# A two-layer decoder on one core: two evictions given to VectorE around silu, a context rounding a round later, the gated feed-forward layer transposed, unread matmuls in the last division

## The chip, the cores and the metric

The kernel runs on 1 core of one Trainium2 chip. The metric is device time in microseconds (us). Before the change it is 509.97 us, the median of 3 runs (506.48 to 510.33).

## What is computed

Two decoder layers over x of 8 batches x 56 tokens x 256 features. The parts of the reference that matter here, cut:

```python
# layer 0, cross attention over ctx_2048 (8 x 1500 x 256), 16 heads of 16
q, k, v = proj(hs, Wq, bq, S), proj(at, Wk, bk, T), proj(at, Wv, bv, T)
scores = clip(einsum('bhsd,bhtd->bhst', q, k) / 4, -50, 50)   # masked keys: -50
probs = softmax(scores)
delta = einsum('bhst,bhtd->bhsd', probs, v) @ Wo.T + bo
# layer 0, gated feed-forward, 256 -> 1024 -> 256, on quantised activations and ternary weights
gate = einsum('bsh,oh->bso', act_quant(x), weight_quant(w_gate))
up   = einsum('bsh,oh->bso', act_quant(x), weight_quant(w_up))
intermediate = silu(gate) * up
out = einsum('bsh,oh->bso', act_quant(fwht(intermediate)), weight_quant(w_down))
# act_quant: per token, scale = 128 / max|x|, round, clip; fwht: Walsh-Hadamard over 1024
```

Ahead of it stands self attention of layer 0 (16 heads of 128); behind it attention of layer 1 across the batches, a summary of the context, and a second feed-forward layer (h, a lookup of gelu, out).

## The kernel before

The 448 tokens are four divisions of 112 (`NT`, `TT`), t = 0 to 3; each holds two batches. Each engine runs a program written out by hand, with semaphores between them.

**Stages.** Warm-up matmuls and the first normalisation (to about 9 us of the span), self attention of layer 0 over 16 heads (to about 130 us), then the cross attention in 48 rounds (`PAIRS`), s = 0 to 47, of 250 context rows each; two rounds make a unit u = s // 2 of 500 rows, six rounds a batch. What stands behind cross attention for division t (its output projection, the gated feed-forward, layer 1) is cut into steps and woven into the rounds: `early(t, o)` and `late(t, o)` run step o of division t in round s = 12(t + 1) + o. Division 3 has no rounds left, so its steps, with what is left of divisions 0 to 2, make a serial last stretch from 428 us to the end.

**A round on TensorE (PE).** `scores(s)` (L1469, into `psa`); `project_k` for the next unit (L1398, into the bank `kvb` of `psb`); `weighted_values(s - 1)` (L1487, into `pvb`); early steps; `project_vu` for the next unit (L1408, also into `kvb`); late steps. As keys and values use one bank, `project_k` waits until the values before have been evicted (`s_vue`), and `project_vu` until the keys have (`s_ke`).

**ScalarE (ACT)** takes `exponential(s)` (L624), `move_k` (L460: keys out of `kvb`), in even rounds `round_up(u + 2)` (L389: the context rounded to fp32r), early steps, `move_vu` (L467: values out of `kvb`), late steps. In rounds 16, 28 and 40 it also runs `silu(t)` for t = 0, 1, 2: it loads another activation table (L502), takes silu of the gate bank (L505), and after `move_vu`, in late step 4, loads the first table back (L508).

**VectorE (DVE)** takes `remainder` (L820: context minus its rounded part, in odd rounds), early steps, `clip(s)` (L983), `weigh` (L959), late steps.

**The gated feed-forward of division t**, before: quantised tokens are transposed (L1520) and evicted (L499, `xqT`); late step 3 (round 15 for t = 0) multiplies them with the gate weights, tokens on the partitions, 4 matmuls of 512 columns (L1526); round 16 takes silu; early step 5 (round 17) multiplies with the up weights (L1526, 4 more; it waits for silu, as it overwrites the gate's banks); late step 5 multiplies both on DVE (`times_up`, L1026); butterflies in rounds 17 and 18 do three of the ten Hadamard stages over blocks of 128 features (L1034, L1035); late step 6 (round 18) transposes the 8 blocks (`turn_inter`, L1547) and ACT evicts them (`move_hT`, L512); early step 7 (round 19) multiplies by the 128 x 128 Hadamard matrix (L1553); the rest (scale, round, down projection) fills rounds 19 to 21. Division 3 does the same in the last stretch in halves (L1706, L1712, L662, L1229, L1720, L669, L1726).

`keep_warm(n)` issues n matmuls of 128 x 512 (L1678) whose result nobody reads.

## Time and profile before

| | |
|---|---|
| runs | 509.97, 506.48, 510.33 us (median 509.97) |
| the profiled execution | 506.57 us, of which the span from first to last instruction is 504.8 us |
| mean granted TensorE clock | 0.993 |
| PE busy | 476.2 us (94%) |
| DVE busy | 357.7 us (71%) |
| ACT busy | 330.3 us (65%) |

How to read it: the span is that of one profiled execution; a matmul's end is modelled, so the distance from one group of matmuls to the next is the better measure of what it costs. The granted clock is the share of full speed at which TensorE was allowed to run: 1.0 is 2.4 GHz and 0.5 is 1.2 GHz. A time in brackets behind a row is how long the engine stood idle before it, with what released it.

### The profile page before, as it was taken

Reading aid. Unit: us, or ns where it says so; the run is one execution under the profiler, and the core shown is the slowest. Engines: PE = TensorE matmul, PEld = TensorE weight load, DVE = VectorE, ACT = ScalarE, POOL = GpSimd, SP = SyncE. Lnnn points to the kernel's source line nnn. Section 1 sums busy time; section 2 is a strip of 40 time slices with the busy share of each in tenths; the row PEclk is TensorE's granted clock in tenths of the full one; section 3 lists DMA queues with packets and bytes.
Section 4 is the critical chain, followed back from the end, with each engine's and each line's share of the span. In section 5 each row is a group of like instructions: output and inputs, shape, how many; then the busy total and the mean of one; then the engine's idle time right before and its main releaser. Section 6 shows DMA issues by size and latency. Waiting matters only on the chain.

```text
span 504.8 us, 16223 instructions
## 1 busy us (share of the span) xinstructions
PE 476.2 (94%) x6980; PEld 404.2 (80%) x6986; DVE 357.7 (71%) x805; ACT 330.3 (65%) x600; POOL 4.2 (1%) x15
## 2 busy tenths in 40 slices
PE   8999999999898999999999998999999899887897
PEld 7999999998787888886878877788877687665575
DVE  5666887888475764673856587955978865698973
ACT  4777787879465656668566667766667756264744
POOL 1000000000000000000000000000000000000000
PEclk9999999999999999999999999999999999799999
DMA  6567451203202111111111111111111100000000
GB/s 195 145 234 258 141 160 39 62 23 123 108 16 70 43 44 44 43 43 43 43 44 43 44 43 43 43 43 44 44 43 44 43 3 3 1 2 1 1 9 29
DMA packets 12236, 30.85 MB, mean 61 GB/s; under 512 B 1667, under 2 KB 4868, under 8 KB 11397
## 3 DMA queue, kind: packets, MB, share of 16 engines
q1 hardware_dynamic: 11716, 29.08, 18.2%
q8 instruction: 56, 0.92, 0.7%
q0 software_dynamic: 192, 0.51, 0.3%
q10 hardware_dynamic: 256, 0.23, 0.1%
q14 instruction: 16, 0.12, 0.1%
HBM read 29.35 MB, written 0.46 MB: 59 GB/s over the span
## 4 chain that ended last, share of the span: by engine, by line
PE 69%; DVE 16%; ACT 10%; issue 4%; DMA 1%; SPq 0%; ACTq 0%; DVEq 0%
PE psb L1408 10%; PE psb L1398 10%; PE psa L1469 8%; PE psa L1317 7%; PE psb L1487 5%; PE psa L1330 4%; PE pst L1339 3%; PE psb L1370 3%; PE psa L1350 2%; ACT shared L624 2%; PE psa L1747 1%; PE pst L1553 1%; PE psb L1361 1%; DVE smem L983 1%; ACT smem L624 1%
## 5 line engine op out<-in xcount | busy, mean ns | idle before, releaser
L1408 PE MATMUL psb<-wkv,cx 128*125 128x256 f32 x576 | 80.4, 288 | 2.8 <-ACT kx L460 2.8
L1398 PE MATMUL psb<-cx,wkv 128*128 128x500 f32 x276 | 74.5, 405 | 4.2 <-ACT vmem L467 4.2
L1408 PEld LDWEIGHTS psb<-wkv,cx 128*125 128x125 f32 x576 | 71.0, 186 | 6.4 <-ACT kx L460 4.9
L467 ACT ACTIVATE vmem<-psb 125x512 f32<-125x512 f32 x48 | 28.6, 596 | 55.9 <-PE psb L1408 55.9
L1398 PEld LDWEIGHTS psb<-cx,wkv 128*128 128x128 f32 x276 | 48.3, 188 | 16.2 <-ACT vmem L467 4.9
L983 DVE TENSOR_SCALAR shared<-shared,top 125x896 f32<-125x896 f32 x48 | 30.8, 684 | 35.8 <-ACT shared L624 35.5
L1469 PE MATMUL psa<-qb,kx 32*125 32x112 f32 x1536 | 54.7, 279 | 0.8 <-ACT shared L624 0.6
L1469 PEld LDWEIGHTS psa<-qb,kx 32*125 32x125 f32 x1536 | 46.3, 183 | 9.3 <-issue 4.6
L983 DVE TENSOR_SCALAR smem<-smem,top 125x896 f32<-125x896 f32 x48 | 30.8, 683 | 27.1 <-ACT smem L624 27.1
L624 ACT ACTIVATE smem<-psa 125x1792 f32<-125x1792 f32 x24 | 40.0, 1666 | 12.3 <-PE psa L1469 12.3
L624 ACT ACTIVATE shared<-psa 125x1792 f32<-125x1792 f32 x24 | 40.0, 1666 | 10.5 <-PE psa L1469 10.3
L1317 PE MATMUL psa<-cx 128*128 128x448 f32 x192 | 43.0, 373 | 0.8 <-DVE cx L792 0.8
L1317 PEld LDWEIGHTS psa<-cx 128*128 128x128 f32 x192 | 34.8, 188 | 3.6 <-DVE cx L792 1.0
L460 ACT ACTIVATE kx<-psb,cols_sb 128x500 f32<-128x500 f32 x46 | 30.9, 672 | 2.3 <-PE psb L1398 2.3
L959 DVE CUSTOM_DVE_ANT_0 scratch<-ring,cw 128x500 f32<-128x500 f32 x48 | 32.3, 673 | 0.0
L373 ACT ACTIVATE shared<-shared,negmax 112x112 f32<-112x112 f32 x64 | 24.1, 378 | 9.2 <-DVE negmax L860 9.2
L820 DVE TENSOR_TENSOR cx<-ring,cx 128x1000 fp32r<-128x1000 f32 x24 | 28.7, 1195 | 2.0 <-ACT cx L389 1.8
L1487 PEld LDWEIGHTS psb<-smem,vmem 125*32 125x32 f32 x1536 | 20.4, 110 | 7.9 <-issue 7.8
L1487 PEld LDWEIGHTS psb<-shared,vmem 125*32 125x32 f32 x1536 | 20.3, 110 | 8.0 <-issue 7.7
L389 ACT ACTIVATE cx<-ring 128x1000 fp32r<-128x1000 f32 x24 | 25.0, 1041 | 2.4 <-DMA ring<-ctx_t_dram 2.4
L1330 PE MATMUL psa<-wkv,cx 128*112 128x256 f32 x192 | 25.2, 280 | 0.0
L1330 PEld LDWEIGHTS psa<-wkv,cx 128*112 128x112 f32 x192 | 24.4, 174 | 0.7
(337 smaller groups left out, 823.9 us busy)
## 6 DMA issues: line engine op xcount, KB each, us to landing
ring<-ctx_t_dram SPq DMA_DIRECT2D x24, 500.0 KB, 3.5
whd<-wqk_dram SPq DMA_DIRECT2D x16, 256.0 KB, 2.7
qb<-wvp_dram SPq DMA_DIRECT2D x8, 256.0 KB, 2.9
whd<-wo_dram SPq DMA_DIRECT2D x16, 128.0 KB, 2.7
wraw<-w_dram SPq DMA_DIRECT2D x2, 1024.0 KB, 5.9
mats_sb<-mats_dram SPq DMA_DIRECT2D x1, 1536.0 KB, 9.0
wraw<-gate_dram SPq DMA_DIRECT2D x1, 1024.0 KB, 6.3
wraw<-up_dram SPq DMA_DIRECT2D x1, 1024.0 KB, 6.9
```

The costliest lines, as they stand in the source:

```text
L460: nc.scalar.activation(kx[u % 2][:, m, :], bank[:, 0:UT], ACT.Identity, bias=cols_sb[:, 1, m:m + 1]).then_inc(s_ke, 1)
L467: nc.scalar.activation(vu[u % 2][:, 2 * r:2 * r + 2, :, 0:XD], bank[0:CT, :].rearrange("p (t h d) -> p t h d", t=2, d=XD), ACT.Copy).then_ ...
L624: nc.scalar.activation(ex[s % 2], psa[0:CT, :, 0:448], ACT.Exp, scale=0.25).then_inc(s_ex, 1)
L820: nc.vector.tensor_tensor(cx[LO][u % 2][:, :, :], ctxs[u % 3], cx[HI][u % 2][:, :, :].bitcast(F32), ALU.subtract).then_inc(s_cx, 1)
L959: nc.vector.tensor_tensor_reduce(out=wscr[:, c, :], in0=ctxs[u % 3][:, c, :], in1=cw[:, (u % UPB) * UT:(u % UPB + 1) * UT], scale=1.0, sca ...
L983: nc.vector.tensor_scalar(half, half, top[:, pp // 2 // UPB, key:key + 1], 1.0 / ECLIP, ALU.min, ALU.max).then_inc(s_clip, 1)
L1317: last = nc.tensor.matmul(PS[0][:, part, 0:TOK], cq[a][h % 2][:, (c * 2 + part) * P:(c * 2 + part + 1) * P], x0[b][:, c, :], start=(a == b ...
L1330: last = nc.tensor.matmul(A2[0:TT, i * D:(i + 1) * D], x0[b][:, c, t * TT:(t + 1) * TT], wkv[a][:, j % 2, c, :], start=(a == b and c == 0) ...
L1398: last = nc.tensor.matmul(bank[:, 0:UT], wkv[a][:, 0, c, m * P:(m + 1) * P], cx[b][u % 2][:, c, :], start=(a == b and c == 0), stop=(a == ...
L1408: last = nc.tensor.matmul(bank[0:CT, t * D:(t + 1) * D], cx[b][u % 2][:, c, a0:a0 + CT], wkv[a][:, 1, c, :], start=(a == b and c == 0), st ...
L1469: last = nc.tensor.matmul(psa[0:CT, g, t * 224 + c * 112:t * 224 + (c + 1) * 112], kx[u % 2][32 * g:32 * g + 32, c, a0:a0 + CT], qb[32 * g ...
L1487: last = nc.tensor.matmul(pvb[32 * i:32 * i + 32, q * S:(q + 1) * S], vu[u % 2][:, 2 * r + t, 4 * q + i, :], ex[pp % 2][:, g, a0:a0 + S], ...
```

## The change

1. **Evictions around silu.** In rounds 16, 28 and 40 (`SILU`) the values, and in the rounds after them (17, 29, 41, `BEHIND`) the keys, are evicted by DVE (`take_vu`, `take_k`) and not by ACT. `round_up` of rounds 16, 28, 40 is done by ACT in the round after, and so is `remainder`, which DVE now does behind `weigh` and not at the round's head.
2. **Transposed layer.** The gate and the up projection now have features on the partitions and tokens in the columns (`widen`: 16 matmuls of 128 x 112 each for the 4 of 512 columns). `turn_inter` and `move_hT` are gone; the Hadamard matmuls read the butterflies' output. The scale of the gate, one number for each token, is now one for each column: `spread_scale` (a matmul) copies it to all partitions, `move_gB` (ACT) evicts it, and `scale_gate` (DVE) multiplies it in and writes the gate to SBUF. So the up projection no longer waits for silu, only for `scale_gate`, and moves from early step 5 to late step 4, a round earlier. The scale of up goes into the quantiser's numbers.
3. **Last division.** The last exponential is cut in two halves; `weighted_values(46)` goes ahead of `project_qkv(2)`; 3 and 4 unread matmuls are added around the transposes of the context; `keep_weighted(7)` goes behind `spread`.
4. **Start.** 18 fp32 warm-up matmuls of 128 x 128 become 6 of these, 8 in fp32r and 16 of 32 x 112; one semaphore (`s_rest`) is merged into another.

```diff
+SILU = (16, 28, 40)
+BEHIND = (17, 29, 41)
...
-        inter = whd[1][0:TT, 0:FF]
-        butt = scratch[0:TT, FF:2 * FF]
+        inter = whd[1][:, 0:FC * TT]
+        butt = scratch[:, FF:FF + FC * TT]
+        gB = sb("gB", [P, TT])
...
+            def move_gB(t):
+                act.wait_ge(s_gb, t + 1)
+                nc.scalar.activation(gB[:, :], (A1 if t == 3 else T1)[:, 0:TT], ACT.Copy).then_inc(s_gbe, 1)
+
             def silu(t):
                 nc.scalar.preload_act_table(ACT.Silu)
-                act.wait_ge(s_gu, t + 1)
-                act.wait_ge(s_gate, t + 1)
-                nc.scalar.activation(sil, both, ACT.Silu, scale=gu[:, t, 0:1]).then_inc(s_sil, 1)
+                act.wait_ge(s_gs, t + 1)
+                nc.scalar.activation(sil, sil, ACT.Silu).then_inc(s_sil, 1)
...
                 exponential(s)
-                if s >= 2 and u + 1 < B * UPB:
+                if s >= 2 and s not in BEHIND and u + 1 < B * UPB:
                     move_k(u + 1, r, kvb)
-                if r == 0 and u + 2 < B * UPB:
+                if (s in BEHIND or r == 0 and s not in SILU) and u + 2 < B * UPB:
                     round_up(u + 2)
...
-                if u + 1 < B * UPB:
+                if s not in SILU and u + 1 < B * UPB:
                     move_vu(u + 1, r, kvb)
...
-            exponential(PAIRS - 1)
+            act.wait_ge(s_qk, PAIRS)
+            act.wait_ge(s_pv, PAIRS - 2)
+            for t in range(2):
+                nc.scalar.activation(ex[1][:, :, t * 224:(t + 1) * 224], psa[0:CT, :, t * 224:(t + 1) * 224], ACT.Exp, scale=0.25).then_inc(s_ex, 1)
...
+            def take_k(u, m):
+                dve.wait_ge(s_kp, 2 * u + m + 1)
+                dve.wait_ge(s_qk, 2 * u - 2)
+                nc.vector.tensor_scalar_add(kx[u % 2][:, m, :], kvb[:, 0:UT], cols_sb[:, 1, m:m + 1]).then_inc(s_ke, 1)
+
+            def take_vu(u, r):
+                dve.wait_ge(s_vp, 2 * u + r + 1)
+                dve.wait_ge(s_pv, 2 * (u - 2) + r + 1)
+                nc.vector.tensor_copy(vu[u % 2][:, 2 * r:2 * r + 2, :, 0:XD], kvb[0:CT, :].rearrange("p (t h d) -> p t h d", t=2, d=XD)).then_inc(s_vue, 1)
...
+            def scale_gate(t):
+                dve.wait_ge(s_gate, t + 1)
+                dve.wait_ge(s_gbe, t + 1)
+                nc.vector.tensor_tensor(in_banks(sil), wide_T, gB[:, :].unsqueeze(1).unsqueeze(1).to_broadcast([P, 2, 4, TT]), ALU.mult).then_inc(s_gs, 1)
...
+                if o == 4:
+                    scale_gate(t)
                 if o == 6:
                     butterfly(t, 1)
...
             for s in range(PAIRS - 2):
-                if s % 2 and s // 2 + 2 < B * UPB:
+                if s in BEHIND:
+                    take_k(s // 2 + 1, 1)
+                elif s % 2 and s // 2 + 2 < B * UPB:
                     remainder(s // 2 + 2)
...
                 weigh(s // 2, s % 2)
+                if s in SILU:
+                    take_vu(s // 2 + 1, s % 2)
+                if s in BEHIND:
+                    remainder(s // 2 + 2)
...
-            for _ in range(18):
+            for _ in range(6):
                 nc.tensor.matmul(T0[:, 0:P], ones[:, :], ones[:, :], start=True, stop=True)
+            for _ in range(8):
+                nc.tensor.matmul(T0[:, 0:P], rounded[:, :], rounded[:, :], start=True, stop=True)
+            for k in range(16):
+                g = 32 * (k % 4)
+                nc.tensor.matmul(PS[k % 4][:, 0, 0:TT], rounded[g:g + 32, :], rounded[g:g + 32, 0:TT], start=True, stop=True, tile_position=(g, 0))
...
+            def spread_scale(t):
+                pe.wait_ge(s_gu, t + 1)
+                if 0 < t < 3:
+                    pe.wait_ge(s_x4d, t)
+                nc.tensor.matmul((A1 if t == 3 else T1)[:, 0:TT], gu[:, t, 0:1].to_broadcast([TT, P]), ident[0:TT, 0:TT], start=True, stop=True).then_inc(s_gb, 1)
+
+            def widen(n, half, bank):
+                for f in range(4 * half, 4 * half + 4):
                     for c in range(DC):
-                        last = nc.tensor.matmul(pst[0:TT, half, :], xqT[:, c, :], wter[:, n, c * FF + half * 512:c * FF + half * 512 + 512],
+                        last = nc.tensor.matmul(bank[:, (f % 4) * TT:(f % 4 + 1) * TT], wter[:, n, c * FF + f * P:c * FF + (f + 1) * P], xqT[:, c, :],
                                                 start=(c == 0), stop=(c == DC - 1))
...
-                if o == 5:
-                    gate_up(t, 1)
...
-                if o == 6:
-                    turn_inter(t)
+                if o == 4:
+                    gate_up(t, 1)
...
+            weighted_values(PAIRS - 2)
             project_qkv(2)
-            weighted_values(PAIRS - 2)
             weighted_values(PAIRS - 1)
+            keep_warm(3)
             turn_context(3)
             nc.tensor.matmul(A3[0:TT, 0:D], minus[:, :], bias2[:, 0:D], start=True, stop=False)
+            keep_warm(4)
             turn_divided(3)
```

The order of the programs around division 1's silu, rounds 28 and 29. ACT before: L624 is the exponential, L460 the keys, L389 `round_up`, L329 and L333 a normalisation's root, L502 and L508 the table loads, L505 silu, L467 the values.

```order
L624 ACTIVATE shared<-psa 125x1792
L460 ACTIVATE kx<-psb,cols_sb 128x500
L389 ACTIVATE cx<-ring 128x1000
L329 ACTIVATE lnv<-mv,eps 112x1
L333 ACTIVATE y<-lnv 112x1
L502 ACT_TABLE_LOAD
L505 ACTIVATE whd<-pst,gu 112x1024
L467 ACTIVATE vmem<-psb 125x32x16
L508 ACT_TABLE_LOAD
L329 ACTIVATE lnv<-mv,eps 112x1
L333 ACTIVATE y<-lnv 112x1
L624 ACTIVATE smem<-psa 125x1792
```

ACT after, the same place (L626 the exponential, L464 the keys, L393 `round_up`, L510 and L515 the table loads, L512 silu, L471 the values).

```order
L626 ACTIVATE shared<-psa 125x1792
L464 ACTIVATE kx<-psb,cols_sb 128x500
L333 ACTIVATE lnv<-mv,eps 112x1
L337 ACTIVATE y<-lnv 112x1
L510 ACT_TABLE_LOAD
L512 ACTIVATE whd<-whd 128x896
L515 ACT_TABLE_LOAD
L333 ACTIVATE lnv<-mv,eps 112x1
L337 ACTIVATE y<-lnv 112x1
L626 ACTIVATE smem<-psa 125x1792
L393 ACTIVATE cx<-ring 128x1000
L471 ACTIVATE vmem<-psb 125x32x16
```

The rounding and the values have left the round of silu, and the next exponential is followed by the rounding and not by the keys.

DVE after, from `clip(28)` to `remainder(16)`, with the short instructions of a normalisation between them left out where the dots stand: L986 `clip`, L960 `weigh`, L997 `take_vu`, L992 `take_k`, L820 `remainder`.

```order
L986 TENSOR_SCALAR shared<-shared,top 125x4x224 x2
L960 ISA scratch,wb<-ring,cw 128x500
L960 ISA wb 128x1
L997 COPY vmem<-psb 125x32x16
...
L992 TENSOR_SCALAR kx<-psb,cols_sb 128x500
L786 SCALAR_TENSOR_TENSOR yt<-y,nx 112x1
L788 SCALAR_TENSOR_TENSOR rs<-yt,y 112x1
L1156 TENSOR_SCALAR wraw<-xs,mv,rs 112x256
L986 TENSOR_SCALAR smem<-smem,top 125x4x224 x2
L960 ISA scratch,wb<-ring,cw 128x500
L960 ISA wb 128x1
L820 TENSOR_TENSOR cx<-ring,cx 128x1000
```

Before, L820 of this unit stood ahead of the same normalisation and of the second `clip`, and the two evictions were not there.

PE before, from the gate matmuls of round 27 to the scores of round 31 (L1469 scores, L1398 keys, L1487 weighted values, L1408 values, L1621 a transpose of layer 1, L1547 `turn_inter`):

```order
L1526 MATMUL pst<-wter,xqT 112x512 x4
L1469 MATMUL psa<-qb,kx 125x112 x16
L1398 MATMUL psb<-cx,wkv 128x500 x6
...
L1487 MATMUL psb<-shared,vmem 32x56 x32
L1526 MATMUL pst<-wter,xqT 112x512 x4
L1408 MATMUL psb<-wkv,cx 125x256 x12
...
L1621 MATMUL pst<-cst,wraw 128x112 x2
L1408 MATMUL psb<-wkv,cx 125x256 x12
L1547 MATMUL pst<-cst,whd 128x112 x8
L1469 MATMUL psa<-qb,kx 125x112 x16
```

PE after (L1506 scores, L1435 keys, L1524 weighted values, L1445 values, L1564 `spread_scale`, L1569 gate and up, L1659 the transpose):

```order
L1564 MATMUL pst<-cst,gu 128x112
L1557 MATMUL pst<-identb,xq 128x112 x2
L1445 MATMUL psb<-wkv,cx 125x256 x12
L1569 MATMUL pst<-xqT,wter 128x112 x16
L1506 MATMUL psa<-qb,kx 125x112 x16
...
L1445 MATMUL psb<-wkv,cx 125x256 x12
L1569 MATMUL pst<-xqT,wter 128x112 x16
L1506 MATMUL psa<-qb,kx 125x112 x16
...
L1659 MATMUL pst<-cst,wraw 128x112 x2
L1445 MATMUL psb<-wkv,cx 125x256 x12
L1506 MATMUL psa<-qb,kx 125x112 x16
```

The second projection has moved from the middle of round 29, between the weighted values and the values, to the end of round 28, and nothing stands between the values and the scores at the end of round 30.

## Rows read from the trace of the kernel before

**Rows 1.** The page's chain that ended last, share of the span by engine.
```profile
PE 69%; DVE 16%; ACT 10%; issue 4%; DMA 1%; SPq 0%; ACTq 0%; DVEq 0%
```

**Rows 2.** Stretches: length, busy us (instructions) of PE, PEld, DVE, ACT, POOL, clock, DMA.
```profile
228.05:253.79 25.74, 24.45 (x486) 20.25 (x485) 16.80 (x30) 17.07 (x17) 0.00 (x0) 1.00 0.17 49
305.92:332.49 26.57, 24.64 (x488) 20.42 (x487) 20.98 (x45) 18.08 (x22) 0.00 (x0) 1.00 0.17 50
305.92:311.06 5.14, 5.14 (x115) 4.32 (x114) 3.83 (x12) 3.88 (x6) 0.00 (x0) 1.00 0.33 103
311.06:319.24 8.18, 6.29 (x119) 4.77 (x118) 5.46 (x15) 6.45 (x8) 0.00 (x0) 1.00 0.01 2
```

**Rows 3.** Timeline of rounds 28 and 29: start us, us, engine, line, operation, [idle before].
```profile
309.25 1.05 ACT L389 ACTIVATE cx<-ring 128x1000 fp32r<-128x1000 f32 x1
310.73 1.28 ACT L502 ACT_TABLE_LOAD   x1
312.02 1.11 ACT L505 ACTIVATE whd<-pst,gu 112x1024 f32<-112x1024 f32 x1
313.03 0.59 ACT L467 ACTIVATE vmem<-psb 125x512 f32<-125x512 f32 x1
313.64 1.28 ACT L508 ACT_TABLE_LOAD   x1
313.68 1.62 PE L1398 MATMUL psb<-cx,wkv 128*128 128x500 f32 x6 [1.47 <-ACT vmem L467]
317.64 1.68 PE L1408 MATMUL psb<-wkv,cx 128*125 128x256 f32 x12 [0.41 <-ACT kx L460]
```

**Rows 4.** Timeline, TensorE: gate of division 1, its two groups of transposes, scores behind.
```profile
304.96 1.02 PE L1526 MATMUL pst<-wter,xqT 128*112 128x512 bf16 x4
...
324.69 0.98 PE L1547 MATMUL pst<-cst,whd 112*128 112x112 f32 x8
325.61 1.14 PE L1469 MATMUL psa<-qb,kx 32*125 32x112 f32 x32
...
338.49 0.57 PE L1560 MATMUL pst<-identb,mats_sb 112*128 112x112 bf16 x8 [0.35 <-DVE mats_sb L1048]
338.99 1.14 PE L1469 MATMUL psa<-qb,kx 32*125 32x112 f32 x32
```

**Rows 5.** Groups by line and form: xcount | busy us, mean ns of one | idle before.
```profile
L815 DVE COPY vmem<-psa 112x512 f32<-112x512 f32 x16 | 11.1, 692 | 6.1 <-PE psa L1330 5.8
L1026 DVE SCALAR_TENSOR_TENSOR scratch<-pst,gu,whd 112x1024 f32<-112x1024 f32 x3 | 3.9, 1284 | 0.1
L1408 PEld LDWEIGHTS psb<-wkv,cx 128*125 128x125 f32 x576 | 71.0, 186 | 6.4 <-ACT kx L460 4.9
```

**Rows 6.** Timeline, VectorE from round 27 to round 29.
```profile
304.43 0.67 DVE L959 CUSTOM_DVE_ANT_0 scratch<-ring,cw 128x500 f32<-128x500 f32 x1
...
307.38 0.42 DVE L1128 TENSOR_TENSOR xs<-xs,rows_sb 112x256 f32<-112x256 f32 x1
...
308.90 1.28 DVE L983 TENSOR_SCALAR shared<-shared,top 125x896 f32<-125x896 f32 x2 [1.10 <-ACT shared L624]
...
312.58 1.20 DVE L820 TENSOR_TENSOR cx<-ring,cx 128x1000 fp32r<-128x1000 f32 x1
```

**Rows 7.** Timeline, last stretch: the same matmuls for division 3 and later.
```profile
436.04 1.91 PE L1766 MATMUL psa<-mats_sb,xnT 128*112 128x256 f32 x4 [0.24 <-issue]
438.06 0.43 DVE L777 BATCH_NORM_STATS2 st<-psa 112x6 f32<-112x256 f32 x1 [2.25 <-PE psa L1766]
...
468.67 1.12 PE L1822 MATMUL psa<-mats_sb,xnT 128*112 128x256 f32 x4
```

**Rows 8.** Stretch of the last part at the lower clock; columns as in group 2.
```profile
434.90:441.60 6.70, 6.46 (x21) 5.01 (x22) 4.10 (x12) 1.94 (x9) 0.00 (x0) 0.50 0.00 0
```

**Rows 9.** Timeline, TensorE at the start: warm-up and first transposes.
```profile
0.99 6.08 PE L1304 MATMUL pst<-ones 128*128 128x128 f32 x36 [0.99 <-POOL magic L304]
7.74 1.12 PE L1299 MATMUL psb<-cst,xn 112*128 112x112 f32 x8 [0.67 <-DVE xn L767]
```

128 lines of the change are left out of this document (55 added, 73 removed).

## The prediction

> **What bounds the kernel now.** I read the page's chain first, then stretches of whole rounds, then the timeline where a round is longer than its neighbours. The chain that ended last runs over TensorE for 69% of the span [rows 1], so a gain must shorten what TensorE issues, or take away a wait of it. In the 48 rounds a plain one takes 5.14 us and TensorE is busy through it; the round behind a silu takes 8.18 us, of which it is busy 6.29 [rows 2]. Round 29 has a plain round's work and the up projection, whose 4 matmuls of 512 columns take 0.96 us (from 304.96 to the next round's start at 305.92) [rows 2, 4]. That is 6.10, so 2.08 us are lost to waits. The timeline names them: ACT runs `round_up` (1.05), a table load (1.28), silu (1.11), only then the values that `project_k` waits for (TensorE idle 1.47), and a second load (1.28) pushes the exponential and the keys back (idle 0.41) [rows 3]. Rounds 28 to 31 take 26.57 us together, 16 to 19 take 25.74 [rows 2]; the work of division 1 in them is that of division 0, so the wait behind silu is 0.83 less there, 1.25 us. Rounds 40 to 43 repeat 28 to 31. Behind 428 us the last stretch runs in small dependent steps.
>
> **Start of the sum.** The profiled execution: 506.57 us. It is one of the fast ones; the runs' median is 3.4 above it.
>
> **1. The transposed layer on TensorE.** Each division loses 8 transposes, 0.92 us from their first to the scores behind [rows 4]. Gate and up become 16 pairs of a 128-column weight load and 112 columns each. Nearest: 8 bf16 transposes of 112 columns, each with its load, take 338.99 - 338.49 = 0.50 us, 62 ns a pair [rows 4], so 1.00 us for 0.96: +0.08 for both. Lower bound: nothing. Upper bound: the fp32r loads of 125 columns, 186 ns each if none overlaps [rows 5]. `spread_scale` is one fp32 matmul of 112 columns; 2 such of 256 take 1.12 us [rows 7], so about 0.2 (bounds 0.1 and 0.5). Together -0.92 + 0.08 + 0.2 = -0.64 us a division. All of it counts, since TensorE is busy there.
>
> What a page says against the transposed form is set apart here. The Trainium skill ("TensorE: Matmul & The Clock Gate", section "Back-to-back issue gap") gives about 81 ns for a matmul of 128 columns with its weight load; the row has 62. By the page's figure the 8 groups of 16 (two in each of four divisions) would cost 8 x 16 x 0.019 = 2.4 us more.
>
> **2. The waits behind silu.** ACT's rounds 28 and 29 lose the values (0.59) and the keys, `round_up` goes behind the second exponential, and silu sees 896 columns. With the values on DVE, `project_k` of round 29 no longer waits for ACT: `clip` and `weigh` of round 28 end before the values are in the bank, and the copy takes 0.69 [rows 5]. Silu hides behind the rest of round 28, as the up projection, now at that round's end, waits for `scale_gate` only. So 1.25 + 2 x 2.08 us go.
>
> What is late next is DVE's queue. I count from the start of round 28 (0); durations without a group are rounded from the same timeline. `scale_gate` waits for the gate and reads 896 columns: 1.28 x 896 / 1024 = 1.12 [rows 5], so it ends at 1.25. Behind it stands layer 1's normalisation of division 0, which before ran from 305.1, where `weigh` ended, to 307.80, 2.7 us [rows 6]: to 4.0. `clip` 1.28, `weigh` about 0.7: to 5.95. `take_vu` waits for values at about 5.1: to 6.6. The next normalisation, about 1.8: to 8.4. Round 29 starts at 5.14 + 1.0 = 6.15, and its keys are there at 6.15 + 1.07 + 1.55 = 8.8 (scores and keys as in the timeline of every plain round); `take_k` to 9.6, just when the weighted values end (9.75), so no wait. ACT's root for that normalisation ends only at about 8.7, and its exponential (1.67) behind it at 10.4, where before it began at once. `clip`, `weigh`: to 12.4. `remainder` 1.20 [rows 6]: to 13.6. But `project_k` of round 30, which reads it, could start at 6.15 + 5.15 + 1.07 = 12.4. I therefore charge a new wait of 1.15 us in rounds 30 and 42, bounds 0 (if the normalisations slip into gaps) and 2.1 (the old wait in full). In round 18 no normalisation of an earlier division is in the way: the same count ends at 12.8 against 12.4, and I charge 0.5.
>
> DVE's new work (1.12 + 0.69 + 0.7 a division, less an eighth of `times_up` and of six butterflies) is otherwise hidden: DVE is busy 20.98 of 26.57 us in these rounds [rows 2]. It costs once it exceeds the rest, about 5 us.
>
> Loop: divisions 1 and 2: -0.64 - 2.08 + 1.15 = -1.57 each; division 0: -0.64 - 1.25 + 0.5 = -1.39. Sum **-4.5 us**.
>
> **3. The last stretch.** From 434.9 to 441.6 TensorE has half of its clock [rows 8]. There the output projection of division 3 takes 1.91 us where the same shape takes 1.12 later, and DVE waits 2.25 us for it [rows 7]. What the clock did before: TensorE stood with gaps around the context's transposes. The 7 unread matmuls, a quarter of 0.96 us each [rows 4], lie in waits for DVE's `take_raw` and `divide`, so they delay nothing. If the clock stays up, 0.8 us of the projection leave the path, and I estimate 0.45 (between 0 and 0.8) for the small matmuls ahead of it, which ran at the same clock: -1.25. Against it `scale_gate` stands in two halves behind the wide `total` on DVE, +1.1, and gives back an eighth of the product and the butterflies, -0.65; the transposes' eviction was hidden by DVE. Halved exponential and earlier weighted values: -0.1. That is -0.9 with the clock up, rounded to **-1.0 us**, and +0.35 without; I take -1.0, since the added matmuls stand just ahead of the fall.
>
> **4. The start.** Shorter warm-ups gain nothing: TensorE waits for `xn`, ready at 7.74 whatever it did before [rows 9]. Merging a semaphore takes no instruction away but a wait. Price: 0, upper bound in rival C.
>
> **Sum.** 506.57 - 4.5 - 1.0 = 501.07, so **501.0 us**. The median of the runs shown is 509.97, 1.8% above that; a cause of their two levels (506.5 and 510) is not in this profile, and I don't forecast that it goes.
>
> **Rivals.**
> - **A, DVE's queue takes the whole gain.** `take_k` and `take_vu` are queued in order behind normalisations that wait for ACT; if keys or values come late as well as the remainder, each division keeps its old wait, and only the removed transposes are left: 506.57 - 3 x 0.64 - 1.0 = 503.6; with more waits in rounds 17 to 19, up to 507. For: the count above has 0.2 us of slack at the keys. Against: DVE is busy 5.46 of 8.18 us in round 29 [rows 2].
> - **B, weight loads don't overlap (slower).** At p ns a pair the 8 groups cost 128 x (p - 62). The point of no gain is 5.5 us / 128 + 62 = 105 ns. At the 186 ns of the fp32r load [rows 5] it is +15.9, so 517. Against: the loads in rows 4 do overlap, with bf16 weights as here.
> - **C, a slow start.** The warm-ups end some 2 us earlier (6 of 18 fp32 matmuls are 2.0 of 6.08 us; the 24 others are short), so TensorE idles about 2.5 us rather than 0.67 before its first transposes [rows 9]. If it then has half its clock as long as in rows 8, some 5.5 us of matmuls take 1.7 times as long (1.91 / 1.12): +3.9 at most, 504.9; half hidden, 503.
> - **D, the change doesn't do what it says**: the clock falls in the last stretch all the same: 502.4.
>
> **How the numbers follow.** The forecast with D (one answer): 0.58, between 497.5 (no new wait: 3.0 less, and some of the lost time elsewhere) and 503.5. A 0.18, 503 to 507. C 0.14, 502 to 505. B 0.10, of which half above 515. The range 497 to 507 leaves out B and a little at the low end: also in it is a median on the upper of the two levels (501 + 3.4 = 504.5). About 1% is what a measurement of this kernel can tell from no change; against 509.97 faster means below 504.9: the forecast nearly whole, C's larger and A's smaller part, 0.76. Within 1%: 0.18. Slower: 0.06.
>
> **What would show it.** In the changed profile: rounds 17, 29 and 41 at 5.2 us, rounds 16, 28 and 40 at 6.2; `project_k` of rounds 30 and 42 waiting about 1.1 us for DVE's `remainder` (none in A's place would be a gain more; waits for `take_k` or `take_vu` speak for A); 16 matmuls of the gate in 1.0 us (B: over 1.7); no `turn_inter`; a granted clock of 1.0 around 435 us (D: 0.5) and from 7 to 12 us (C: 0.5). I am wrong if the 12 rounds around the silus together are not 3 to 7 us shorter than their 78.9.

## The result, and the profile of the changed kernel

| | before | changed |
|---|---|---|
| median, us (executions) | 506.44 (20) | 504.10 (20) |
| lowest to highest | 504.98 to 510.33 | 502.77 to 506.83 |
| profiled execution | 506.57 | 502.77 (span 501.0) |
| first scores of the loop | 140.38 | 142.20 |
| loop, first to last scores | 286.30 | 281.38 |
| last scores to the end of the span | 78.1 | 77.4 |

The ratio is 0.995, with a 95% interval of 0.9929 to 0.9972. The changed kernel is 2.3 us (0.5%) faster; forecast was 5.5 us below before's profiled execution, 501.0. The three executions of before shown ahead of the forecast had a median of 509.97; twenty give 506.44, so that 3.5 of the 9 us between 510 and 501 were never there; of the other 5.4 us the change brought 2.3. The profiled executions differ by 3.8 us, and the table's lower rows say where: loop -4.92, last stretch -0.7, start +1.82.

The chain that ended last, by engine, answers to [rows 1]: ACT has lost half of its share to TensorE and DVE.

```profile
PE 71%; DVE 18%; ACT 5%; issue 4%; DMA 1%; DVEq 0%; ACTq 0%
```

Rounds 28 to 31 of the changed kernel, as stretches (length, then busy us of PE, PEld, DVE, ACT, POOL, clock, DMA share, GB/s), answering to [rows 2]:

```profile
306.25:312.20 5.95, 5.95 (x132) 5.12 (x131) 5.56 (x14) 4.68 (x6) 0.00 (x0) 1.00 0.28 85
312.20:317.39 5.19, 5.19 (x117) 4.33 (x115) 4.32 (x13) 4.44 (x6) 0.00 (x0) 1.00 0.02 5
317.39:323.74 6.35, 5.33 (x117) 4.48 (x116) 6.18 (x12) 4.13 (x5) 0.00 (x0) 1.00 0.28 83
323.74:330.91 7.17, 6.95 (x131) 6.05 (x130) 6.98 (x14) 2.84 (x3) 0.00 (x0) 1.00 0.08 10
sum 24.66, PE 23.42 PEld 19.99 DVE 23.05 ACT 16.09 POOL 0.00; mean PE 5.86 PEld 5.00 DVE 5.76 ACT 4.02 POOL 0.00
```

They take 24.66 us for 26.57. Round 29 has lost its 2.08 us of waits. What waits now is round 30, and DVE is busy through 23.05 of the 24.66 us, where it was 20.98 of 26.57. The timeline of the same rounds names the operations, answering to [rows 3] and [rows 4]:

```profile
311.31 0.96 PE L1569 MATMUL pst<-xqT,wter 128*128 128x112 bf16 x16
311.42 0.95 ACT L512 ACTIVATE whd<-whd 128x896 f32<-128x896 f32 x1
313.27 1.62 PE L1435 MATMUL psb<-cx,wkv 128*128 128x500 f32 x6
...
319.55 1.58 PE L1435 MATMUL psb<-cx,wkv 128*128 128x500 f32 x6 [1.02 <-DVE cx L820]
...
326.66 0.99 PE L1524 MATMUL psb<-shared,vmem 125*32 125x56 f32 x64 [0.22 <-DVE craw L977]
```

`project_k` of round 29 (313.27) waits for nothing; that of round 30 (319.55) waits 1.02 us for DVE's `remainder`. New besides is a small wait in round 31 for `take_raw` (L977, the context's copy `craw`).

At the start the changed kernel's first matmuls are slower than those of [rows 9]. Timeline of TensorE, then the stretch behind its warm-ups:

```profile
0.99 2.93 PE L1336 MATMUL pst<-ones 128*128 128x128 f32 x12 [0.99 <-POOL magic L308]
3.57 1.95 PE L1338 MATMUL pst<-ones 128*128 128x128 f32 x8
...
7.67 1.73 PE L1330 MATMUL psb<-cst,xn 112*128 112x112 f32 x8 [1.11 <-DVE xn L768]
10.12 4.13 PE L1354 MATMUL psa<-cx 128*128 128x448 f32 x12 [0.72 <-ACT cx L362]
```

```profile
7.40:14.00 6.60, 5.61 (x20) 4.92 (x21) 3.63 (x8) 4.09 (x8) 1.77 (x3) 1.00 0.65 199
```

The transposes take 1.73 us for 1.12 and the first 12 matmuls of `project_qk` 4.13 for 2.77. The granted clock of the stretch is shown as 1.00 all the same. That is no record: the first record of the clock in this trace begins at 13.34 us of the span (in the kernel before at 4.78 us), and the view counts time without a record as full speed. The distances between the starts of instructions say what the clock was. In the changed kernel's fp32 and rounded warm-ups they are 0.21 us to the end, and in `project_qk` 0.37 us up to 13.3 us and 0.20 behind it; in the kernel before, those of the warm-ups fall from 0.21 to 0.11 us at 4.8 us. So the changed kernel's TensorE was not at full speed in its warm-ups, which end at 6.55 us, nor before 13.3 us.

In the last stretch the clock no longer falls at 434.9 [rows 8], 8.2 us behind the last scores, but at 440.0, 16.4 us behind them, over gate and up of division 3. The output projection, then the gate, then both stretches:

```profile
432.25 1.02 PE L1787 MATMUL psa<-mats_sb,xnT 128*112 128x256 f32 x4
433.38 0.43 DVE L778 BATCH_NORM_STATS2 st<-psa 112x6 f32<-112x256 f32 x1 [0.41 <-PE psa L1787]
440.25 1.67 PE L1569 MATMUL pst<-xqT,wter 128*128 128x112 bf16 x16 [0.45 <-ACT xqT L503]
```

```profile
434.90:439.90 5.00, 3.10 (x22) 2.04 (x20) 4.51 (x17) 2.90 (x7) 0.00 (x0) 1.00 0.01 2
440.20:443.60 3.40, 3.35 (x35) 3.35 (x35) 3.13 (x7) 1.54 (x3) 0.00 (x0) 0.53 0.00 0
```

The projection takes 1.02 us for 1.91, and DVE waits 0.41 us for it, not 2.25 [rows 7].

### The profile page after: what moved, and what is told of

It reads as the page before. It is cut to its first block, busy times and chain, and to the rows that moved or that the text cites. A ratio compares the mean times of both kernels' runs of the same rounds, so it can differ in the third digit from the quotient of the medians.

```text
span 501.0 us, 16404 instructions
## 1 busy us (share of the span) xinstructions
PE 474.7 (95%) x7067; PEld 406.3 (81%) x7067; DVE 363.4 (73%) x817; ACT 324.2 (65%) x594; POOL 4.3 (1%) x15
## 4 chain that ended last, share of the span: by engine, by line
PE 71%; DVE 18%; ACT 5%; issue 4%; DMA 1%; DVEq 0%; ACTq 0%
PE psb L1445 11%; PE psb L1435 10%; PE psa L1506 8%; PE psa L1354 7%; PE psb L1524 6%; PE psa L1367 4%; PE pst L1376 4%; PE psb L1407 3%; PE psa L1387 2%; ACT shared L626 2%; PE psa L1766 1%; PE pst L1569 1%; DVE scratch L960 1%; PE pst L1591 1%; DVE shared L986 1%
## 5 line engine op out<-in xcount | busy, mean ns | idle before, releaser
L1445 PE MATMUL psb<-wkv,cx 128*125 128x256 f32 x576 | 80.2, 288 | 2.2 <-ACT kx L464 2.2
L1435 PE MATMUL psb<-cx,wkv 128*128 128x500 f32 x276 | 74.4, 405 | 2.5 <-DVE cx L820 2.2
L1445 PEld LDWEIGHTS psb<-wkv,cx 128*125 128x125 f32 x576 | 71.0, 186 | 4.7 <-ACT kx L464 2.9
L471 ACT ACTIVATE vmem<-psb 125x512 f32<-125x512 f32 x45 | 26.8, 596 | 53.3 <-PE psb L1445 53.3
L1435 PEld LDWEIGHTS psb<-cx,wkv 128*128 128x128 f32 x276 | 48.3, 188 | 14.4 <-issue 2.7
L1506 PE MATMUL psa<-qb,kx 32*125 32x112 f32 x1536 | 54.7, 279 | 0.8 <-ACT shared L626 0.6
L986 DVE TENSOR_SCALAR shared<-shared,top 125x896 f32<-125x896 f32 x48 | 30.8, 685 | 31.5 <-ACT shared L626 31.2
L1506 PEld LDWEIGHTS psa<-qb,kx 32*125 32x125 f32 x1536 | 46.3, 183 | 8.2 <-issue 3.4
L626 ACT ACTIVATE smem<-psa 125x1792 f32<-125x1792 f32 x23 | 38.4, 1669 | 12.8 <-PE psa L1506 12.8
L626 ACT ACTIVATE shared<-psa 125x1792 f32<-125x1792 f32 x24 | 40.0, 1665 | 10.4 <-PE psa L1506 10.1
L1354 PE MATMUL psa<-cx 128*128 128x448 f32 x192 | 44.4, 382 | 0.7 <-ACT cx L362 0.7
L986 DVE TENSOR_SCALAR smem<-smem,top 125x896 f32<-125x896 f32 x48 | 30.8, 682 | 19.1 <-ACT smem L626 18.5
L1354 PEld LDWEIGHTS psa<-cx 128*128 128x128 f32 x192 | 36.1, 195 | 3.7 <-DVE cx L793 1.0
L960 DVE CUSTOM_DVE_ANT_0 scratch<-ring,cw 128x500 f32<-128x500 f32 x48 | 32.3, 673 | 0.0
L464 ACT ACTIVATE kx<-psb,cols_sb 128x500 f32<-128x500 f32 x43 | 28.9, 673 | 4.2 <-PE psb L1435 3.9
L820 DVE TENSOR_TENSOR cx<-ring,cx 128x1000 fp32r<-128x1000 f32 x24 | 28.7, 1195 | 1.9 <-ACT cx L393 1.8
L1524 PEld LDWEIGHTS psb<-shared,vmem 125*32 125x32 f32 x1536 | 20.4, 110 | 9.0 <-issue 6.7
L1524 PEld LDWEIGHTS psb<-smem,vmem 125*32 125x32 f32 x1536 | 20.3, 110 | 8.0 <-issue 7.8
L393 ACT ACTIVATE cx<-ring 128x1000 fp32r<-128x1000 f32 x24 | 24.9, 1037 | 2.4 <-DMA ring<-ctx_t_dram 2.3
```

The lines of the kernel that those rows point to most:

```text
L464: nc.scalar.activation(kx[u % 2][:, m, :], bank[:, 0:UT], ACT.Identity, bias=cols_sb[:, 1, m:m + 1]).then_inc(s_ke, 1)
L471: nc.scalar.activation(vu[u % 2][:, 2 * r:2 * r + 2, :, 0:XD], bank[0:CT, :].rearrange("p (t h d) -> p t h d", t=2, d=XD), ACT.Copy).then_ ...
L626: nc.scalar.activation(ex[s % 2], psa[0:CT, :, 0:448], ACT.Exp, scale=0.25).then_inc(s_ex, 1)
L820: nc.vector.tensor_tensor(cx[LO][u % 2][:, :, :], ctxs[u % 3], cx[HI][u % 2][:, :, :].bitcast(F32), ALU.subtract).then_inc(s_cx, 1)
L960: nc.vector.tensor_tensor_reduce(out=wscr[:, c, :], in0=ctxs[u % 3][:, c, :], in1=cw[:, (u % UPB) * UT:(u % UPB + 1) * UT], scale=1.0, sca ...
L986: nc.vector.tensor_scalar(half, half, top[:, pp // 2 // UPB, key:key + 1], 1.0 / ECLIP, ALU.min, ALU.max).then_inc(s_clip, 1)
```

## The experiments

Times are medians, with lowest, highest and number of executions; ratios are to the kernel before on the same chip, whose median there was 506.40 to 506.69. "Changed" is the kernel of the result. "12 rounds" are 16 to 19, 28 to 31 and 40 to 43 together.

| kernel | us | ratio, 95% | loop starts | loop | 12 rounds |
|---|---|---|---|---|---|
| before | 506.44 | | 140.38 | 286.30 | 78.9 |
| changed | 504.10 | 0.995 | 142.20 | 281.38 | 73.2 |
| e1_old_warmup | 501.37 (500.64 to 502.53, 6) | 0.9877 to 0.9923 | 140.37 | 281.41 | 73.2 |
| e2_before_new_warmup | 508.28 (507.39 to 511.08, 12) | 1.0022 to 1.0059 | 142.28 | 285.98 | 78.9 |
| e4_layer_only | 506.34 (505.70 to 509.61, 12) | 0.9981 to 1.0017 | 142.47 | 283.07 | 75.0 |
| e5_evictions_only | 504.88 (503.97 to 507.89, 12) | 0.9956 to 0.9992 | 140.48 | 284.84 | 77.6 |
| e3_no_unread | 503.33 (501.31 to 507.29, 12) | 0.9905 to 0.9956 | 140.35 | 285.00 | 73.2 |
| e7_more_unread | 502.75 (501.01 to 505.46, 8) | 0.9890 to 0.9944 | 140.46 | 285.14 | 73.2 |
| e6_dve_order | 501.63 (501.48 to 504.17, 6) | 0.9878 to 0.9938 | 140.42 | 281.74 | 72.2 |
| e9_short_warmup | 506.19 (502.27 to 507.71, 10) | 0.9933 to 0.9994 | 142.91 | 284.19 | 73.2 |
| e8_long_rounded | 505.25 (500.48 to 506.26, 8) | 0.9902 to 0.9975 | 145.10 | 281.02 | 73.2 |
| e11_filled_wait | 503.36 (502.14 to 504.11, 6) | 0.9912 to 0.9961 | 142.64 | 281.51 | 73.2 |
| e12_split_wait | 501.59 (501.12 to 501.78, 4) | 0.9865 to 0.9931 | 140.34 | 281.27 | 73.2 |
| e13_all | 499.29 (499.10 to 499.85, 5) | 0.9833 to 0.9883 | 140.37 | 279.69 | 70.1 |

### The start: e1 and e2

```diff
 pe.wait_ge(s_init, 1)
-for _ in range(6):                      # fp32, then 8 + 16 rounded ones
+for _ in range(18):                     # fp32 only, as before
     nc.tensor.matmul(T0[:, 0:P], ones[:, :], ones[:, :], start=True, stop=True)
```

`e1_old_warmup` is the changed kernel with the old warm-ups; `e2_before_new_warmup` the kernel before with the new ones.

> The changed kernel with the 18 fp32 warm-up matmuls of before; all else as changed. Theory (the start pays): in the changed kernel's trace the first 8 transposes take 1.73 us and not 1.12, and the first values of self attention start at 14.09 us and not 12.31; with the old warm-ups they are back near 12.3, the loop's first scores near 140.4, and the time falls by about 1.8 us against the changed kernel. Rival (the late start is chance, or comes from another edit such as the merged semaphore): the first values still start near 14.1 in part of the executions, and the median stays within 0.5 us of the changed kernel's 504.1.

> The kernel before with the changed kernel's warm-ups (6 fp32, 8 fp32r, 16 of 32 x 112); all else as before. Theory (the start pays): the first transposes take about 1.7 us, the first values start near 14.1 us, and the time rises by about 1.8 us over before. Rival (chance, or another edit): no change beyond 0.5 us.

The timeline of TensorE in e1:

```profile
7.71 1.07 PE L1330 MATMUL psb<-cst,xn 112*128 112x112 f32 x8
9.62 2.78 PE L1348 MATMUL psa<-cx 128*128 128x448 f32 x12 [0.84 <-DVE cx L793]
```

The start is the old one, and e1 takes 501.37 us, 2.7 less than the changed kernel. In e2 the transposes take 1.73 us and the loop starts at 142.28; the kernel before becomes 1.7 us slower. So the new warm-ups cost 1.8 to 1.9 us at the loop's start in a profiled execution, with either loop, and the rest of the change is worth the 5.2 us that lie between 506.59 (before beside e1) and 501.37.

### Length or kind of the warm-ups: e9 and e8

```diff
-for _ in range(18):                     # e9: fp32 alone, but shorter
+for _ in range(11):
```

```diff
 for _ in range(6): ...                  # e8: fp32, as in the changed kernel
-for _ in range(8):                      # rounded, 128 columns
+for _ in range(28):
     nc.tensor.matmul(T0[:, 0:P], rounded[:, :], rounded[:, :], start=True, stop=True)
-for k in range(16): ...                 # the small ones
```

> The changed kernel with 11 fp32 warm-up matmuls: the old kind of work, which ends at about the time at which the new mixture ended (6.5 us), so that TensorE idles as long ahead of its first transposes. If the idle time ahead of the transposes is what lowers the clock, the first transposes take 1.7 us for 1.1 and the loop's first scores stand at 142.2 as in the changed kernel (504.1 - about 503.5 us). If the kind of the warm-ups counts (the 24 small ones), the start is as in e1: transposes 1.07, loop's first scores 140.4, 501.4 us.

> The changed kernel with warm-ups of the new kind (6 fp32 matmuls, then fp32r ones: 28 instead of 8, and none of the 16 small ones), so that they last as long as the old ones. If the idle time ahead of the first transposes is the cause of the slow start, this start is the old one: transposes 1.07 to 1.12 us, first values at 12.2 to 12.3, the loop's first scores at 140.4, 501 to 501.7 us. If the kind counts (the row of the changed kernel shows a granted clock of 1.00 there, though its matmuls take 1.5 times as long), transposes stay at 1.73 and the loop's first scores at about 142.2.

TensorE in e9, where it stands idle for 2.04 us, and its stretch behind:

```profile
7.71 1.27 PE L1330 MATMUL psb<-cst,xn 112*128 112x112 f32 x8 [2.04 <-DVE xn L768]
```

```profile
8.60:15.30 6.70, 5.97 (x19) 5.06 (x19) 3.16 (x6) 3.67 (x8) 0.70 (x2) 0.50 0.72 222
```

TensorE in e8, where it is not idle at all, and its stretch behind:

```profile
3.58 6.21 PE L1338 MATMUL pst<-ones 128*128 128x128 f32 x28
9.59 1.72 PE L1330 MATMUL psb<-cst,xn 112*128 112x112 f32 x8
```

```profile
9.40:14.00 4.60, 3.88 (x15) 3.35 (x15) 2.31 (x5) 2.01 (x4) 0.00 (x0) 1.00 0.58 196
```

Each theory shows in a kernel of its own. In e9 the warm-ups reach full speed at 5.1 us, TensorE then stands idle for 2.04 us, and the clock falls at 8.5 us, during the transposes: with warm-ups at full speed, idle time alone makes the start slow. (The median of e9 is no price of this. Its executions stand in two groups, four at 502.3 to 503.1 us and six at 506.1 to 507.7, and the profiled one, of the upper group, loses time in round 2 as well, as told below.)

In e8 there is no idle time, and the transposes take 1.72 us nevertheless; the 28 rounded matmuls started 0.21 us apart, so they themselves ran slowly to their end at 9.8 us (which also delayed the transposes by 1.9 us, for which I had not allowed: I had taken their price from too short a row). The first record of the clock begins at 17.2 us there, so the 1.00 of its stretch is again no record. Of e8's eight executions three took 500.5 to 500.7 us and five 504.6 to 506.3. One of the five was profiled; that the three reached full speed in their warm-ups fits their times, but is not shown.

In the nine profiles with fp32 warm-ups alone, full speed was reached at 4.8 to 7.0 us. In the five with rounded ones it was reached at 3.9 us once (e11, below), and otherwise not before 13.2 us. As the changed kernel's warm-ups end at 6.55 us, within the range of the nine, it may be enough that they are short; that their kind matters too rests on e8 alone.

### What the unread matmuls of the last division do: e3 and e7

```diff
 weighted_values(PAIRS - 1)
-keep_warm(3)                            # e3: neither
 turn_context(3)
 ...
-keep_warm(4)
 turn_divided(3)
```

```diff
-keep_warm(4)
+keep_warm(8)                            # e7: longer, and 2 more
 spread_scale(3)
+keep_warm(2)
 turn_xq(3)
```

Both on top of e1.

> The changed kernel with the old warm-ups (as e1_old_warmup, 501.37 us) and without the 3 + 4 unread matmuls of the last division. If those hold the clock there, as I forecast, the granted clock falls earlier, near 435 us on the old count, and the output projection of division 3 takes 1.9 us for 1.1: the forecast's terms (-1.25 with the clock held, none without) give up to +1.25, so 501.7 to 502.6. In the changed kernel the clock fell anyway, at about 440 us, for 3.4 us of the records; if the unread matmuls only shift a fall that comes in any case, the fall is longer or sits over other work, and I expect +0.3 to +0.8. Rival: they change nothing, since TensorE's gaps ahead of the fall come from other places; then within 0.2 us of e1 and the same stretches at half clock.

> The changed kernel with the old warm-ups and two longer blocks of unread matmuls: 8 for 4 while DVE normalises ahead of the gate of division 3, and 2 more behind spread_scale(3). In the changed kernel TensorE stands idle from about 437.2 to 440.2 and is then at half clock until about 443.8; gate and up of division 3 take 1.67 and 1.70 us there, where 16 such pairs take 0.8 to 1.0 in the loop. If the idle time ahead brings the fall, the clock stays up over gate and up: about 0.7 of each pair of stretches, of which the up projection hides partly behind DVE's scale_gate, so -0.5 to -0.9 us against e1's 501.37. Rival: the added matmuls run past the moment at which the gate could start (8 of a quarter of 0.96 us are 1.9 us), and delay what they should help: 0 to +0.5.

Stretches around gate and up of division 3 and, for e1 and e7, some 14 us later. First e1, then e3, then e7:

```profile
438.40:441.80 3.40, 3.40 (x48) 3.40 (x49) 3.30 (x8) 1.81 (x3) 0.00 (x0) 1.00 0.00 0
452.80:456.40 3.60, 3.29 (x17) 2.48 (x18) 2.89 (x7) 1.97 (x4) 0.00 (x0) 0.61 0.01 2
```

```profile
441.90:445.40 3.50, 3.47 (x36) 3.48 (x37) 3.40 (x8) 1.88 (x3) 0.00 (x0) 0.56 0.00 0
```

```profile
442.20:445.60 3.40, 3.39 (x48) 3.39 (x49) 3.30 (x8) 1.80 (x3) 0.00 (x0) 1.00 0.00 0
455.60:459.00 3.40, 2.66 (x16) 2.23 (x17) 2.71 (x6) 2.39 (x5) 0.00 (x0) 0.56 0.01 2
```

In each profile of the new last division the clock falls for 3.4 us once or twice there: over the gate, some 14 us later, or at both places, as in e3, whose second fall is at 456.0 us. The unread matmuls don't decide where. The changed kernel, e8, e11, e12 and e13 have the last division of e1, and their clock falls over the gate as it does in e3; in e12 it falls at both places. Its stretch over the gate:

```profile
439.40:442.70 3.30, 3.30 (x26) 3.30 (x24) 3.20 (x8) 2.61 (x4) 0.00 (x0) 0.50 0.00 0
```

Nor does the place matter much: `scale_gate` begins 17.49 to 17.53 us behind the last scores in e1, e3 and e7, whether the gate takes 0.96 or 1.36 us, since the last stretch is DVE's there. From the last scores to the end it is 77.7 us in e1, 78.1 in e3, 78.0 in e7. But the profiles with e1's own last division run from 77.3 us (e11, e13) to 78.4 (e12), so neither taking the unread matmuls away nor adding more has an effect that these profiles could tell from nothing. My expectation of -0.5 to -0.9 for e7 was wrong: it took the changed kernel's slow gate as given, and in e1 the gate ran in 0.96 us without the added matmuls.

In e3 the projection takes 1.02 us as in the changed kernel, so it isn't the 7 unread matmuls of the last division that moved the fall away from 434.9. Nor is it the warm-ups: in e2 the clock falls 8.2 us behind the last scores, as before. What did lies in the part of the change that e4 has and e5 has not (both below), as the stretch behind 434 us shows, first of e5, then of e4:

```profile
433.30:440.20 6.90, 6.90 (x24) 5.21 (x24) 4.41 (x12) 2.26 (x9) 0.00 (x0) 0.52 0.00 0
```

```profile
433.50:440.50 7.00, 5.76 (x37) 4.32 (x37) 5.96 (x21) 3.65 (x11) 0.00 (x0) 1.00 0.01 2
```

That is the rewritten last division, and within it, by e3, not the 7 matmuls; the halved exponential, the earlier weighted values and the later `keep_weighted(7)` are what is left ahead of that place, untested.

The medians of e3 and e7 are 1.4 to 2 us above that of e1, and their profiled executions 4. Almost all of the 4 us is one place outside the change, which the next section treats.

### Round 2, and the spread between executions: e11

In the profiles of e3 and e7 rounds 2 and 3 take 3.6 and 3.7 us more than in e1. The reason stands in the timelines: a transfer of the context lands late, ACT's rounding behind it too, and TensorE waits longer for ACT's `xnT`. ACT begins that rounding at 153.12 us in e1 and 0.55 us later in e3. ACT and TensorE in e3, and TensorE's stretch behind:

```profile
153.67 1.04 ACT L393 ACTIVATE cx<-ring 128x1000 fp32r<-128x1000 f32 x1 [2.92 <-DMA ring<-ctx_t_dram]
155.01 1.54 PE L1457 MATMUL pst<-xnT,mats_sb 128*128 128x112 f32 x8 [2.07 <-ACT xnT L478]
```

```profile
155.60:161.60 6.00, 6.00 (x59) 4.64 (x62) 4.13 (x12) 1.92 (x2) 0.00 (x0) 0.50 0.01 3
```

In the kernel before this wait was 1.53 us, in the changed one 1.49, in e1, e2, e4, e5 and e6 1.29 to 1.50 (later in e8 1.12, in e12 1.32), and the clock stayed; in e3, e7 and e9 it was 2.02 to 2.17, and the clock fell. In these three ACT's rounding begins some 0.6 us later than in e1, counted from the loop's first scores, and rounds 2 and 3 together take 2.1 to 3.7 us more.

```diff
+if s == 2:
+    pe.wait_ge(s_ex, 3)
+    for _ in range(5):                  # unread, into a bank of the scores
+        nc.tensor.matmul(A0[:, 0:P], ones[:, :], ones[:, :], start=True, stop=True)
 if s in (2, 4, 6):
     project_q(s // 2)
```

> The changed kernel as it is (with its own warm-ups), with 5 unread fp32 matmuls of 128 columns (0.27 us each) in the wait of round 2, ahead of project_q(1), in which TensorE waits 1.3 to 1.5 us for ACT's xnT. In the ten profiles so far, the seven with a wait of 1.53 us or less kept the clock there, and the three with 2.02 to 2.17 us lost it for about 9 us and 2 to 3.6 us of time; half of the changed kernel's executions ran above its profiled one. Theory: those are executions in which round 2 lost its clock; the filled wait keeps it, and the median falls from 504.1 to 502.7 to 503.2, with no execution above 504. Rival: the spread comes from the start (V0 at 14.1 to 14.4 us or later), and the median stays at 503.8 to 504.4 with executions up to 506.

TensorE in e11, at the start and in round 2, and the stretch behind its warm-ups:

```profile
3.58 1.23 PE L1338 MATMUL pst<-ones 128*128 128x128 f32 x8
7.71 1.73 PE L1330 MATMUL psb<-cst,xn 112*128 112x112 f32 x8 [2.32 <-DVE xn L768]
156.69 1.15 PE L1463 MATMUL pst<-xnT,mats_sb 128*128 128x112 f32 x8 [0.35 <-ACT xnT L478]
```

```profile
7.40:14.00 6.60, 5.56 (x18) 4.85 (x19) 3.67 (x8) 4.14 (x8) 1.76 (x3) 0.50 0.65 199
```

The median is 503.36 and no execution is above 504.11, where the changed kernel reached 506.83. The median fell by 0.7, half of what the theory gave at best, with the highest slightly above my 504; with six executions it speaks for the theory and doesn't prove it. Nor does the profile: the rounding began 12.7 us behind the loop's first scores there, as in e1, and not 13.3 as in e3, so this was not an execution in which the wait would have been long. That a filled wait keeps the clock when the transfer is late isn't shown. The start shows why something is left: here the warm-ups did speed up (the same 8 rounded matmuls take 1.23 us for 1.95, with full speed from 3.9 us on), so they ended earlier, TensorE idled 2.32 us, and the clock fell to 0.50, this time on record. Slow warm-ups or a longer gap behind fast ones: the first transposes take 1.73 us either way.

### The layer and the evictions apart: e4 and e5

```diff
 for s in range(PAIRS - 2):              # e4, ACT: as before the change
-    if s >= 2 and s not in BEHIND and u + 1 < B * UPB:
+    if s >= 2 and u + 1 < B * UPB:
         move_k(u + 1, r, kvb)
-    if (s in BEHIND or r == 0 and s not in SILU) and u + 2 < B * UPB:
+    if r == 0 and u + 2 < B * UPB:
         round_up(u + 2)
```

```diff
 for s in range(PAIRS - 2):              # e5, DVE: on the kernel before
-    if s % 2 and s // 2 + 2 < B * UPB:
+    if s in BEHIND:
+        take_k(s // 2 + 1, 1)
+    elif s % 2 and s // 2 + 2 < B * UPB:
         remainder(s // 2 + 2)
```

`e4_layer_only` has the transposed layer, the new last division and the new warm-ups, but evictions, rounding and `remainder` where they were; `e5_evictions_only` is the kernel before with just these moved.

> The changed kernel with all evictions, roundings and remainders where they were before (ACT evicts, the remainder at the head of the odd round); the transposed layer stays. Theory (two parts of like size): the transposed layer alone takes the up projection out of the wait for silu, but the values and keys still wait behind silu on ACT: rounds 29 and 41 at about 7.0 us (8.18 less the up projection's 0.96 and a little of the wait), 28 to 31 together about 25.8, so some 2.5 us slower than the changed kernel over the loop. Rival (the layer does it all): silu at 0.95 us rather than 1.11 and an earlier start leave rounds 28 to 31 at 24.7 as in the changed kernel.

> The kernel before with only the evictions, roundings and remainders moved as in the change; the layer is not transposed. Theory: the up projection of round 29 still waits for silu, which ends 1.05 us earlier without the rounding ahead of it, and the keys no longer wait behind it: rounds 28 to 31 about 25.5 us for 26.57, the loop about 3 us shorter than before. Rival (the evictions alone bring nothing, as DVE's queue returns the wait at the remainder): 26.2 or more.

TensorE in e4, round 29, and in e5, round 30:

```profile
314.45 0.72 PE L1429 MATMUL psb<-cx,wkv 128*128 128x500 f32 x2 [0.49 <-ACT vmem L471]
...
318.41 1.68 PE L1439 MATMUL psb<-wkv,cx 128*125 128x256 f32 x12 [1.42 <-ACT kx L464]
```

```profile
318.25 1.58 PE L1416 MATMUL psb<-cx,wkv 128*128 128x500 f32 x6 [0.60 <-DVE cx L822]
...
323.73 0.99 PE L1565 MATMUL pst<-cst,whd 112*128 112x112 f32 x8 [1.22 <-DVE whd L1047]
```

The layer alone leaves 1.91 us of waits in round 29, as values and keys still stand behind silu on ACT: rounds 28 to 31 take 25.37 for 26.57, less by the missing transposes and some 0.3. The evictions alone empty round 29 (5.96) and fill round 30 (8.14): they move the wait to DVE's `remainder` and to the butterflies, whose output the transposes read. In the loop the layer is worth 3.23 us and the evictions 1.46; together it is 4.92. The parts nearly add up, but the order of the reasons is other than I had it: the evictions alone gain 0.44 us a division, because a wait that is only moved is there again. My 25.5 us for rounds 28 to 31 of e5 was wrong (26.14); the rival's "26.2 or more" came within 0.1, for its reason.

### Is the wait for the remainder a matter of order: e6, e12, e13

```diff
 clip(s)                                 # e6, DVE
+if s in BEHIND:
+    remainder(s // 2 + 2)
 weigh(s // 2, s % 2)
-if s in BEHIND:
-    remainder(s // 2 + 2)
```

In e6 `take_raw` also goes ahead of `clip` in rounds 18, 30 and 42.

```diff
-pe.wait_ge(s_cx, u + 1)                 # e12, project_k
-for a, b in PARTS:
+pe.wait_ge(s_ch, u + 1)
+for a, b in PARTS0:
+    if b == LO:
+        pe.wait_ge(s_cx, u + 1)
```

> The changed kernel with the old warm-ups and two moves in DVE's order: remainder ahead of weigh in rounds 17, 29 and 41, and take_raw ahead of clip in rounds 18, 30 and 42. The changed kernel waits 1.02 us for the remainder in round 30 (row: PE L1435, DVE cx L820) and 0.29 for the raw context in round 31; rounds 18 and 19 are 0.2 and 0.5 longer than their neighbours of the same work. If each wait is only a matter of order, all go: 3 x about 1 to 1.3 us less the half that comes back as other waits, so -1.5 to -2.5 us against e1's 501.37, with round 30 at 5.3 to 5.6 for 6.35. Rival: DVE's whole queue is what is late in those rounds, and what was passed (weigh, clip) holds up the weighted values instead: then only 0 to -0.7 us, and the wait stands at L1448 or L1439, for weigh or take_k, in round 30 or 31.

> The changed kernel with the old warm-ups, in which project_k takes the two parts that read the rounded context first and waits for DVE's remainder only ahead of the third. That takes the wait of 1.02 us in rounds 30 and 42 off TensorE's way (two parts last 1.08 us). If the wait was a matter of order, rounds 30 and 42 fall from 6.35 to 5.35 and round 18 by 0.2: -2.2 us against e1's 501.37. Rival: DVE is the bound of rounds 28 to 31 (busy 23.05 of 24.66 us; 6.98 of 7.17 in round 31), and what round 30 gains round 31 gives back as a longer wait for clip or the raw context, because DVE still ends there at the same time: round 30 at 5.4, round 31 at about 8.0, sum of both within 0.3 of 13.5, and 501.0 to 501.6 us.

> Best version: the changed kernel with the old warm-ups, the split wait of e12_split_wait, the filled wait of e11_filled_wait, and the copy of the raw context (0.39 us on DVE) moved to ACT in rounds 18, 30 and 42, where ACT is busy 4.1 of 6.35 us. If DVE is the bound of these rounds, each division gains the 0.39 that DVE sheds and little more: 3 x 0.4 = -1.2 against e1, 500.2. If the waits were a matter of order only, -2.2 - 0.9: 498.3. If ACT's copy is in the way of its keys or values, nothing or +0.5: 501.4 to 502.

e12 as two stretches, rounds 30 and 31, with the wait in round 31:

```profile
315.42:320.82 5.40, 5.40 (x117) 4.41 (x117) 5.26 (x11) 4.05 (x5) 0.00 (x0) 1.00 0.31 98
320.82:328.94 8.12, 6.96 (x131) 6.06 (x130) 7.90 (x15) 2.94 (x4) 0.00 (x0) 1.00 0.06 11
```

```profile
324.67 0.99 PE L1520 MATMUL psb<-shared,vmem 125*32 125x56 f32 x64 [1.16 <-DVE craw L977]
```

This is the rival to the number: round 30 gains its 1.0 us, round 31 gives 1.0 back, the sum is 13.52 for 13.52 in the changed kernel, and 501.59 us stand beside e1's 501.37. The wait of 1.02 us was only the place at which DVE's lateness showed.

e6 shortens round 30 to 5.76 and round 42 to 5.78. In division 2 it gives this back through a transfer. `weigh` is the last reader of the ring's slot; with `remainder` ahead of it the slot comes free later and SyncE issues the next transfer 1.3 us later. The issue in round 42 of e1; then in e6 that issue, and ACT's rounding and TensorE in round 43:

```profile
393.63 0.33 SPq L296 DMA_DIRECT2D ring<-ctx_t_dram  x1
```

```profile
394.92 0.33 SPq L296 DMA_DIRECT2D ring<-ctx_t_dram  x1
398.97 1.04 ACT L393 ACTIVATE cx<-ring 128x1000 fp32r<-128x1000 f32 x1 [2.22 <-DMA ring<-ctx_t_dram]
400.79 1.63 PE L1431 MATMUL psb<-cx,wkv 128*128 128x500 f32 x6 [0.99 <-ACT vmem L471]
```

ACT waits 2.22 us for the transfer with the values queued behind it, and round 43 takes 7.96 for 7.17. In divisions 0 and 1 it comes back mainly as waits for ACT's keys, which grow from 0.41 to 1.02 us in round 20 and from 0.43 to 0.76 in round 32. The 12 rounds are 0.9 us shorter, but round 20 stands outside them and takes 7.51 for 6.55, and the loop is 0.3 us longer than e1's. Neither my -1.5 to -2.5 us nor the rival's 0 to -0.7 came.

e13 takes work off DVE instead: ACT copies the raw context in rounds 18, 30 and 42.

```diff
+if s - 1 in BEHIND:                     # ACT, ahead of root
...
+    act.wait_ge(s_pv, 2 * UPB * (b + 1))
+    act.wait_ge(s_ct, b // 2)
+    nc.scalar.activation(craw[...], pvb[...], ACT.Copy).then_inc(s_ce, 1)
```

It has the old warm-ups and the split and filled waits too. Its rounds 30 to 32:

```profile
314.93:320.32 5.39, 5.39 (x118) 4.41 (x117) 5.25 (x11) 3.90 (x5) 0.00 (x0) 1.00 0.31 98
320.32:327.20 6.88, 6.88 (x132) 6.05 (x131) 6.81 (x13) 3.24 (x6) 0.00 (x0) 1.00 0.01 2
327.20:334.49 7.29, 5.77 (x123) 4.73 (x123) 4.41 (x11) 5.46 (x6) 0.00 (x0) 1.00 0.24 70
```

Rounds 30 and 31 have no wait left (TensorE is busy in all 12.27 us), round 32 gets 0.7 us of it back as a wait for ACT's keys; 0.54 us a division remain, some more than the 0.39 that DVE sheds. Expected were 500.2 us with DVE as the bound and 498.3 with the waits a matter of order; 499.29 lies between them. At 499.29 us, 1.4% below before, this is the best version; of its 7.1 us the two waits' edits were not timed apart from the copy.

## Why the prediction failed where it did

- **Start (item 4), the step that failed.** "Price: 0", since TensorE "waits for `xn`, ready at 7.74 whatever it did before". It still does (7.67), but what runs behind the wait is slower. It costs 1.82 us in the profiled execution and 2.7 between the medians of e1 and the changed kernel. Rival C had the size (502 to 505), with a chance of 0.14, and in part by luck. Its mechanism, a longer idle time behind warm-ups at full speed, is that of e9 and e11 (2.04 and 2.32 us). In the changed kernel's own profile the warm-ups never reached full speed: the 6 fp32 matmuls took 2.6 us where C counted 2.0, and the idle time was 1.11 us, not 2.5. C's sign, a granted clock of 0.5 from 7 to 12 us, reads 1.00 there for want of a record. [rows 9] held a warning: a gap of 0.67 us at full speed, and nothing at all on a longer one, nor on warm-ups that end sooner.
- **Loop (items 1 and 2), right.** Forecast -4.5, measured -4.92; the 12 rounds fell from 78.9 to 73.2, within the 3 to 7 us named. The transposes are gone, and 16 pairs take 0.96 us, 60 ns each, for the 62 taken. Rounds 17, 29 and 41 are 5.2 us as forecast, 16, 28 and 40 5.95 for 6.2. The new wait in rounds 30 and 42 was forecast at 1.15 and is 1.02; round 18 is 0.25 longer, for 0.5. Not forecast: 0.2 to 0.4 us for `take_raw` in rounds 19, 31 and 43. `spread_scale` costs 0.23 for 0.2. (The 81 ns a pair that the Trainium skill gives in "TensorE: Matmul & The Clock Gate", section "Back-to-back issue gap", are not what this kernel shows, where a pair has 112 columns; an estimate from that figure is 1.3 us for a group of 16.)
- **What the wait meant, wrong.** I charged it as one late `remainder`. e12 shows DVE's whole queue to be the bound, as rival A had it, though at a price of some 1.2 us a division (1.02 in round 30 and 0.22 in round 31) rather than of all. The sum was right because the count of DVE's queue from which it came was right.
- **Last stretch (item 3), right in sum only.** Forecast -1.0, measured -0.7. DVE's centring starts 1.58 us earlier (forecast 1.25), and 0.7 of it are given back by the end of the butterflies (forecast 0.45). But the clock fell later instead of staying up, and e3 and e7 show no worth of the unread matmuls. The -0.7 is that of one pair of profiles: the three with the old last division have 78.0 to 79.0 us there, the nine with the new one as it is 77.3 to 78.4.
- **The sum.** 506.57 - 4.92 - 0.7 + 1.82 = 502.77, the profiled execution. With the start as I priced it, e1 measures 501.37 where the forecast's sum was 501.07.
- **The comparison, the other step that failed.** The chance of 0.76 for faster rested on 509.97, a median of three. Of the 1.8% that the forecast lay below it, 0.7 are that median's height over 506.44. Against 506.44 even the forecast's own 501.0 is 1.1% faster, hardly beyond what a measurement can tell, and rival C's times are within 1%. Two of three executions happened to be high; the profiled one, near the twenty's median, was the better guide; it was used for the sum and not for this comparison.
- **From 502.77 to 504.10.** The profiled execution was the lowest of twenty. Part of the rest may be round 2's clock, of which the one profile of before shows nothing; e11 speaks for it and doesn't prove it.

## What to carry to other kernels

A gap in TensorE's work is priced by the speed of what follows, not by its length: ask what runs in the first microseconds behind each gap that a change lengthens, above all at the start and where a transfer ends the wait. Read from the distances between matmuls whether the warm-up reached full speed at all, as a clock column can lack a record there. When an engine is busy nine tenths of a stretch, a wait for it that disappears comes back a round later; take work off the engine rather than reorder it, and look which transfer the reordered instruction releases. And compare a forecast with a median only when it is one of many executions.

## What the runs showed of the hardware

- The view's granted clock reads 1.00 where the trace has no record of it: 1.73 us for transposes that take 1.12, with 1.00 shown, in the changed kernel (first record at 13.34 us) and e8 (1.72 us; first record at 17.21 us), and the same 1.73 us with 0.50 on record in e11. Where a start has records, they agree with the distances between instructions, as in e11, where these fall from 0.21 to 0.11 us at the first record (3.87 us). The Trainium skill ("TensorE: Matmul & The Clock Gate", section "Seeing it yourself") says that these trace events have been seen to be unreliable. What these starts show is records that are missing, not false ones.
- What TensorE did before it reached full speed: in e8 rounded (fp32r) matmuls of 128 columns ran without a gap from 3.58 to 9.8 us and stayed 0.21 us apart; in e11 the same ones came to 0.11 us at 3.9 us. With fp32 matmuls alone, full speed came at 4.8 to 7.0 us in all nine profiles, and the first transposes took 0.93 to 1.12 us in the eight whose warm-ups ended within 0.7 us of them.
- Two gaps of nearly the same length in round 2, up to 1.5 us in nine profiles and 2.0 to 2.2 us in three, differed by 2.1 to 3.7 us in what followed.
- A fall of the clock at the end of the program stood 8.2 to 8.3 us behind the last scores with the old last division (in e5 a second one at 32), and 16 to 18 us, 30 to 32 us or both with the new one, with and without unread matmuls. It was absent from no profile.
